# Keys of a context's first row tile by TensorE's transposes instead of a transposing transfer

## The reference

```python
def reference(x, ctx, ...):
    x = x + self_attention(layernorm(x))
    q, k, v = layernorm(x), ctx, ctx             # 16 heads of 64, no projections
    scores = einsum('bhqd,bhkd->bhqk', qh, kh) / sqrt(64)
    attn = softmax(where(causal, scores, -10000))
    x = x + einsum('bhqk,bhkd->bhqd', attn, vh)
    xn = layernorm(x)
    idx, weight = argmax, max of softmax(xn @ Wr.T + br)
    return x + (B[idx] @ (A[idx] @ xn)) / 64 * weight
```

## Time and profile before

| | |
|---|---|
| median of 3 runs | 2275.24 us |
| lowest and highest | 2269.47 and 2275.5 us |
| the profiled execution | 2272.91 us |
| its span, first to last instruction | 2270.8 us |
| mean granted TensorE clock | 0.970 |
| TensorE matmul busy | 2054.8 us (90% of the span) |
| VectorE, ScalarE, GpSimd busy | 1640.1, 1173.8, 975.2 us |
| the hardware queue's share of 16 DMA engines | 72.0% |

### The profile page before, as it was taken

How to read it: one execution, slowest core, us unless ns; L and a number is a source line. 1 busy time by engine, 2 the same in 40 slices (tenths; PEclk the granted TensorE clock), 3 DMA queues, 4 the chain that set the end, 5 groups by cost and what they waited for, 6 DMA issues and landing times. The chain is left out here.

```text
span 2270.8 us, 52078 instructions
## 1 busy us (share of the span) xinstructions
PE 2054.8 (90%) x19320; PEld 1327.4 (58%) x19320; DVE 1640.1 (72%) x4595; ACT 1173.8 (52%) x3114; POOL 975.2 (43%) x919
## 2 busy tenths in 40 slices
PE   1657899999999999999999999997689999999978
PEld 1435666666666666666666666665355555555544
DVE  8877678777777777787777777766566767667664
ACT  6976434333433433333333333334676868687851
POOL 4333334333333343333343333323465656566641
PEclk9778999999999999999999999997899999999989
DMA  9977665665657566656565566568999999999952
GB/s 245 194 158 149 139 142 134 144 143 134 152 124 161 134 135 145 143 129 158 128 155 138 137 142 142 127 151 206 220 198 222 220 223 220 226 220 227 210 119 72
DMA packets 801532, 372.83 MB, mean 164 GB/s; under 512 B 747512, under 2 KB 747768, under 8 KB 801280
## 3 DMA queue, kind: packets, MB, share of 16 engines
q1 hardware_dynamic: 801280, 369.50, 72.0%
HBM read 104.11 MB, written 49.28 MB: 68 GB/s over the span
## 5 line engine op out<-in xcount | busy, mean ns | idle before, releaser
L108 ACT ACTIVATE prob<-prob,negmax 128x128 f32<-128x128 f32 (+1 forms) x1024 | 428.5, 444 | 190.7 <-DVE negmax L101 190.1
L905 POOL TENSOR_TENSOR halves<-prob,halves 128x384 f16<-128x384 f32 x256 | 239.0, 934 | 586.0 <-ACT halves L829 586.0
L71 PE MATMUL ps_j<-xT,wT 128*128 128x256 f16 x3634 | 414.9, 275 | 22.7 <-DMA wT<-rows_qkv 22.7
L101 DVE CUSTOM_DVE_ANT_0 prob<-ps_s,mask 128x128 f32<-128x128 f32 (+1 forms) x1024 | 304.4, 353 | 165.3 <-PE ps_s L91 161.8
L71 PEld LDWEIGHTS ps_j<-xT,wT 128*128 128x128 f16 x3634 | 358.0, 99 | 82.6 <-issue 23.0
L1062 DVE TENSOR_TENSOR raw<-raw,cos 128x512 f32<-128x512 f32 x128 | 137.7, 1076 | 248.6 <-DMA swp<-raw 248.6
L818 ACT ACTIVATE raw<-ps_j,factor_qk 128x256 f32<-128x256 f32 x158 | 66.1, 469 | 450.5 <-PE ps_j L71 450.5
L1600 POOL TENSOR_TENSOR halves<-prob,halves 128x768 f16<-128x768 f32 x128 | 210.5, 1644 | 155.9 <-ACT halves L1550 155.9
L71 PE MATMUL ps_t<-xT,wT 128*128 128x256 f16 x2254 | 255.9, 274 | 0.0
L71 PEld LDWEIGHTS ps_t<-xT,wT 128*128 128x128 f16 x2254 | 221.4, 98 | 36.7
L71 PE MATMUL ps_j<-wT,yT 128*128 128x512 f16 x897 | 203.5, 382 | 0.0
(11 more groups left out here) (194 smaller groups left out, 3589.8 us busy)
## 6 DMA issues: line engine op xcount, KB each, us to landing
swp<-raw SPq DMA_DIRECT2D x512, 64.0 KB, 2.0
xin<-in_x SPq DMA_DIRECT2D x33, 512.0 KB, 4.4
x_kept<-after_self_attention SPq DMA_DIRECT2D x32, 512.0 KB, 4.4
xres<-in_x SPq DMA_DIRECT2D x31, 512.0 KB, 4.3
after_self_attention<-xres SPq DMA_DIRECT2D x30, 512.0 KB, 3.3
queries<-q2T SPq DMA_DIRECT2D x30, 512.0 KB, 3.1
kv_ahead<-in_ctx SPq DMA_DIRECT2D x30, 512.0 KB, 5.1
out<-x SPq DMA_DIRECT2D x20, 512.0 KB, 4.1
```

The costliest lines, as they stand in the source:

```text
L71: last = pe.matmul(out, lhs(t[0], a), rhs(t[1], a), start=a == 0 and t is terms[0], stop=a == n_tiles - 1 and t == (0, 0))
L101: dve.tensor_tensor_reduce(scores[:, cols], bank[:, cols], hidden, scale, NO_SCORE, ALU.add, ALU.min, least[:, n:n + 1]).then_inc(done, 1)
L108: last = act.activation(prob[:, cols], prob[:, cols], ACT.Exp, scale=-1.0, bias=least[:, n:n + 1], accum_out=None if sums is None else sum ...
L905: pool.tensor_tensor(halves[:, e, 1, :], prob[:, e], halves[:, e, 0, :], ALU.subtract).then_inc(prob_lo, 1)
```

## The change

In steps 2 and 4 of round r TensorE transposes four blocks each of the float32 context tile `kv[:, 0]` of batch r + 1 into a bank (`key_transposes`, a new kind `k` in the lists, with the offset -1 for the batch ahead); ScalarE takes the high halves at the start of steps 3 and 5 (`HIGH_AHEAD`), VectorE the low ones as the last thing of `LAST[3]` and `LAST[5]`. SP issues one keys' transfer a round instead of two, that of row tile 1 in step 5. `ctx_in` becomes one semaphore a row tile, `load_context` waits for the key transposes of the batch before, too, and `scores` at a round's start waits for the two low halves.

```diff
              (("h", 1, 2, FIRST), ("t", 0, 2, None)),
-             (("h", 1, 2, SECOND),),
+             (("h", 1, 2, SECOND), ("k", 0, -1, None)),
              (("e", 0, 2, None), ("t", 1, 2, None)),
-             (("e", 1, 2, None),),
+             (("e", 1, 2, None), ("k", 1, -1, None)),
...
-    HIGH_AHEAD = ((), (), (("t", 0, 2),), (), (("t", 1, 2),), (),
+    HIGH_AHEAD = ((), (), (("t", 0, 2),), (("k", 0, -1),), (("t", 1, 2),), (("k", 1, -1),),
...
-            (("e", 0, 2),),
+            (("e", 0, 2), ("k", 0, -1)),
             (("t", 1, 2), ("e", 1, 2)),
-            (("e", 2, 2),),
+            (("e", 2, 2), ("k", 1, -1)),
...
-            return kT_in[b % 2], 16 * NT * ((b + 1) // 2)
+            return kT_in[b % 2], 16 * ((b + 1) // 2)
...
                     sp.wait_ge(v_done, 2 * (b - 1))
-                sp.dma_start(kv[:, n], ctx_t[b][:, n]).then_inc(ctx_in, 16)
+                    sp.wait_ge(j_ready, ready(("k", b - 1, 1)))
+                sp.dma_start(kv[:, n], ctx_t[b][:, n]).then_inc(ctx_in[n], 16)
...
-                if s in (4, 5) and b + 1 < NB:
-                    transpose_keys(b + 1, s - 4)
+                if s == 5 and b + 1 < NB:
+                    transpose_keys(b + 1, 1)
...
+            def key_transposes(b, k):
+
+                to = claim(("k", b, k))
+                if k == 0:
+                    pe.wait_ge(ctx_in[0], 16 * b)
+                for a in range(4):
+                    last = pe.transpose(to[:, bass.ts(a, P)], kv[:, 0, bass.ts(4 * k + a, P)],
+                                        ident[:])
+                last.then_inc(j_ready, 1)
...
                     pe.wait_ge(*keys_in(b))
+                    for k in range(2):
+                        pe.wait_ge(*freed(("k", b, k)))
...
+                if kind == "k":
+                    return kT[:, b % 2, 0, bass.ts(k, 4), 0:P]
...
-                act.wait_ge(ctx_in, 16 * NT * b)
+                act.wait_ge(ctx_in[n], 16 * b)
...
+                    if kind == "k":
+                        low(kT[:, b % 2, 1, bass.ts(k, 4), 0:P],
+                            kT[:, b % 2, 0, bass.ts(k, 4), 0:P], ("k", b, k))
```

More of the change, by code:

```diff
@@ L1246, in second_half @@
         qh_last = sb("qh_last", [P, NT, 2, D], F16)
-        ctx_in, x1_in = sem("ctx_in"), sem("x1_in")
+        ctx_in = [sem(f"ctx_in{n}") for n in range(NT)]
+        x1_in = sem("x1_in")
         kT_in = [sem(f"kT_in{k}") for k in range(2)]
@@ L1298, in halves_done @@
         def halves_done(c):
-            return len([o for o in order[:place[c] + 1] if o[0] in "xt"])
+            return len([o for o in order[:place[c] + 1] if o[0] in "kxt"])
         def transposed(g):
@@ L1496, in _ @@
                 for kind, b, k, part in listed(EXTRA, g):
-                    if kind == "x":
+                    if kind == "k":
+                        key_transposes(b, k)
+                    elif kind == "x":
                         pe.wait_ge(ln_done, 2 * b + 2)
@@ L1510, in high @@
                 act.wait_ge(j_ready, ready(c))
-                act.activation(dst, bank(c)[:], ACT.Copy).then_inc(hi_done, 1)
+                act.activation(dst, bank(c)[:].rearrange("p (a n) -> p a n", a=dst.shape[1]),
+                               ACT.Copy).then_inc(hi_done, 1)
             def pair(k):
```

## The result

| | before | with the change |
|---|---|---|
| median | 2274.03 us (8 runs, 2269.47 to 2275.5) | 2280.67 us (8 runs, 2279.01 to 2285.68) |
| the profiled execution, its span | 2272.91, 2270.8 us | 2280.01, 2278.2 us |
| mean granted TensorE clock | 0.970 | 0.971 |

The ratio is 1.0029, with a 95% interval of 1.0020 to 1.0037: 6.6 us slower. That is 0.29%, at the edge of what I called no change, and the interval leaves out zero. The forecast was 2284.5, 3.8 more, and the time lies in its range (1.2 of the 3.8 is that the median of before, over more runs, came out lower than the 2275.24 that I had). The direction holds; of the terms, the largest had the wrong cause, as the rows show.

A forecast was written before the change was run, and what follows sets the result against it. TensorE was taken as the bound, delayed one for one by VectorE's chain between residual sum and maxima. 9.9 + 2.0 - 2.6 + 0 = +9.3 us on 2272.91 gave 2282.2, or 2284.5 as a median; range 2272 to 2295.

The forecast's parts named there:

- The largest term: Steps 2 to 5 of 13 rounds: step 4's maxima come 0.76 us later each round, 9.9 us in all.
- Step 2, 4 transposes, 0.43; net 0.16 with the 0.27 of step 3: TensorE: four more transposes cost 0.43 us; step 3's wait of 0.27 absorbs part, delaying its product by 0.16.
- VectorE, step 3, 0.60: One more subtraction between residual sum and statistics delays step 4's maxima by 0.60 us, with nothing to hide it.
- ScalarE, "hidden": ScalarE's added copy in step 3, 0.5 us, falls ahead of exponentials whose next ones wait for VectorE, so costs nothing.
- Step 4, 0.43 hidden: TensorE's four more transposes in step 4, 0.43 us, are hidden by the longer VectorE chain; otherwise they cost 0.09.
- Banks, hidden: The last four of sixteen transposes reuse step 5's keys bank, free in time by 0.2 us; otherwise some 0.1.
- ScalarE's copy of step 5, transfer 0.5 later: It delays step 5's exponentials and the remaining keys' transfer by 0.5 us; 8 late starts add 2.0 in all.
- Round 14, -2.6: The load of sums is issued 2.03 us earlier and lands 0.56 faster without keys ahead: gain 2.6, bounds 2.0 to 4.6.
- Rounds 0 and 1, 0: The 5.00 us keys' wait at round 1's start was taken as unchanged, 0, with bounds -5.0 and +2.
- The queue is relieved: Rival: fewer transposing transfers clear the keys' waits at round starts; -5.7 us, so 2269.5; chance 0.24.
- All starts wait: Rival: the 0.5 us counts fully and instruction packets meet keys' transfers in all 13 rounds; 2297 us; chance 0.08.
- The clock falls: Rival: a longer wait before the sixteen transposes lowers TensorE's clock, some 2.5 us a round; 2317 us; chance 0.05.

The follow-up runs named there:

- e1: The change, with VectorE's subtraction moved from the end of step 3's list to the head of step 4's; 2280.2 us, ratio 1.0021.
- e2: e1, with ScalarE's copy of step 3 also moved behind that step's exponentials; 2275.24 us, ratio 0.9999.
- e4: The change, with its keys' transfer issued ahead of the probabilities' transfer of step 5; 2271.75 us, ratio 0.9985.
- e5: The kernel before, with both keys' transfers issued ahead of the probabilities' transfers of steps 4 and 5; 2264.85 us, ratio 0.9957.
- e3: The kernel before, with the load of the sums ahead of the keys' transfer of step 4 in round 14; 2270.94 us, ratio 0.9979.
- e7: The change, with the keys' copy of step 3 made by VectorE ahead of its subtraction, not by ScalarE; 2302.26 us, ratio 1.0119.

## Why the prediction was right, and where it was wrong

The direction and the two smaller terms were right for their reasons. The largest term, 9.9 us, was near by luck: another mechanism gave 5.8, and one stray round of the profiled run 2.1. By the prediction's own sign, "I am wrong if rounds are less than 0.5 longer", its account of the rounds was wrong: undisturbed ones are 0.48 longer, and only late keys and the stray round bring the mean of rounds 2 to 13 to 0.75.

- **Step 2, 4 transposes, 0.43; net 0.16 with the 0.27 of step 3.** The first is exact. The stall that they fill was 0.43, so the net is 0, not 0.16. I took the one idle time that a row names for the whole; comparing step 3 (4.69) with step 1, of nearly the same work (4.26), would have given it.
- **VectorE, step 3, 0.60: the step that failed.** "Nothing hides it" was wrong. A row that the prediction doesn't cite, the small operation of 1.00 us beside its twin of 0.16, hid it: e1 takes the 0.60 away and gains nothing.
- **ScalarE, "hidden".** The copy of step 3 was the cost. It stands in front of exponentials, whose half GpSimd takes, beside which VectorE stands still: 0.48 a round, 5.8 in rounds 2 to 13. e2 returns it. The sum was near because 0.76 and 0.48 are near, with 13 x 0.76 = 9.9 in place of 5.8 + 2.1 for round 10; the 2.1 is an accident of the execution, none in e1's trace and twice in e4's.
- **Step 4, 0.43 hidden.** Right: e2's step 4 is 4.26 with them in it, where before has 4.23.
- **Banks, hidden.** Right: the sixteen transposes of round 7 run without a gap.
- **ScalarE's copy of step 5, transfer 0.5 later.** Right: it is issued 4.43 after the scores of step 6, before 3.95. Of 0.5 the late starts paid less: waits beyond a free start grew from 8.5 to 9.7 us, +1.2 for +2.0, in 8 rounds of 3 to 14 as before, though in part not the same ones. That packets make a start late fits all of them; e5 shows the other half of the cause, the place in the queue.
- **Round 14, -2.6.** It gained 2.7 with the 0.48 in it, so 3.2; e2, without the 0.48, has 50.04 there, 3.3 less than before. e3 gets 2.8 by the order alone, on a queue that still carries the keys. The mechanism is the queue's order; the size of the removed transfer, over which the prediction weighs two figures, hardly enters.
- **Rounds 0 and 1, 0.** 0.1 in this pair of traces, which shows little: in the other twelve round 2 begins anywhere from 1667.4 to 1673.8 us.
- **Rivals.** *The queue is relieved*: the relief came (0.90 for 0.99) and didn't clear the waits; e5 clears them with no byte fewer. *All starts wait*: 8 of 12. *The clock falls*: not in rounds 2 to 13, but at the start of round 15, for 1.3 us that I had in no term. My reason, that 1.7 is below 1.80, doesn't hold up, since the length of one wait doesn't decide: behind the 2.36 of round 10 the granted clock stayed at 1.00, and behind one of 1.98 it fell in a round of e7 and not in another.

## What to carry to other kernels

Before adding work to an engine on the chain, read the durations of the small operations there, each against its shortest: one that takes six times its shortest is standing still, and it hides what you put ahead of it and charges you for what delays its partner. Then ask of each transfer how much slack its place in the queue leaves, before asking how many bytes could go; here one moved line of the issue order was worth 9 us, and of the 15 removed transfers the runs show a gain from one alone, in round 14, by the place that it left. A remedy has to be tried in the kernel where it will live: the same edit was worth 10.6 us on the change, nothing measurable on the kernel before, and some 8 us there once the keys' transfers stood ahead.

## What the runs showed of the hardware

VectorE's small operation from SBUF to SBUF takes 0.17 us where GpSimd is idle (0.169 at the least, before) and stands still while GpSimd computes, to 0.02 or 0.03 us after its end, for up to 2.07 us. Operations that read PSUM, and the statistics, keep their duration beside the same work (0.69 for L1687, 1.28 for the two of L1658). Others that read two tensors in SBUF show it too: the gate's difference L1704, and L1720, 0.64 us beside the same GpSimd operation beside which the reciprocal just ahead of it, L1719, keeps its 0.17. The lines' own rows, of the change (duration in ns, min/median/max):

```profile
L1669 DVE TENSOR_SCALAR rstd<-mv x16: 170/876/2074, 1647.7 to 2242.3; 128x2 f32<-128x2 f32 x16
...
L1704 DVE TENSOR_TENSOR gap<-logit,top x16: 176/726/728, 1666.2 to 2252.2; 128x16 f32<-128x16 f32 x16
...
L1720 DVE TENSOR_TENSOR onehot<-rank,best x16: 156/644/647, 1671.8 to 2253.0; 128x16 f32<-128x16 f32 x16
```

The Trainium skill (SBUF — State Buffer, Who interferes with whom) says that VectorE and GpSimd share one pair of SBUF ports by an exclusive lock, which VectorE's operations with two inputs in SBUF need, and those that use both ports for one input. By that rule the loser waits out the whole instruction of the other, and this case's traces agree, with 0.88 in place of 0.17 us. In each of these rows VectorE is the one that waits. Only the operation that meets GpSimd's is held: at 1647.70 the first of the two small ones began 0.04 us ahead of GpSimd's low half and took 0.17, and its twin behind it took 1.63. GpSimd's rows keep their duration throughout the second half of the change (1.64 to 1.66 us for L1620, 2.13 to 2.14 for L1606), so no run here shows it held.
